# A transformer layer over 16 sequences: the third norm and the first step reordered, and the logarithm of the row sums taken on GpSimd

## The reference

```
x  -> xn = layernorm(x)
q  = xn @ Wq_down.T @ Wq_up.T            c = xn @ Wkv_down.T
k, v per head = c @ k_up[h], c @ v_up[h]
score = q k^T / sqrt(32) - slope[h] * |i - j|, causal
out   = softmax(score) @ v,  then @ Wo.T
x  = x + layernorm(out)
gate, up = layernorm(x) @ w_gu.T  (1408 each; w_gu, w_down decoded from 4-bit codes and scales)
y  = (silu(gate) * up) @ w_down.T;  y = y / rms(y)
x  = x + layernorm(y)
```

## Time and profile before

| | |
|---|---|
| median of 3 runs | 2552.22 us (2552.08 to 2552.81) |
| the profiled execution | 2549.71 us, of which its span is 2547.8 us |
| TensorE (PE) busy | 2445.3 us, 96% of the span |
| VectorE (DVE), ScalarE (ACT), GpSimd (POOL) | 60%, 58%, 23% |
| chain that ended last | PE 80%, DVE 7%, ACT 5%, SP's queue 3% |
| ScalarE table loads | 64 besides the first, 1283 ns each, 4 per step with attention |
| `Ln` of 128x32 | 229 ns, 32 of them |
| `keep_causal` | median 634 ns |
| `h_low` | 1156 ns |

### The profile page before, as it was taken

The page is one execution under the profiler, slowest core; times in us unless marked ns, Lnnn a source line. Parts: engine busy times, 40 slices in busy tenths (PEclk is TensorE's granted clock), DMA queues, the critical chain, the costliest instruction groups (busy, mean ns, idle before and its releaser), DMA issues.

```text
span 2547.8 us, 38721 instructions
## 1 busy us (share of the span) xinstructions
PE 2445.3 (96%) x13372; PEld 1112.6 (44%) x13372; DVE 1523.3 (60%) x4300; ACT 1465.3 (58%) x3927; POOL 591.6 (23%) x648
## 2 busy tenths in 40 slices
PE   6689999999999999999999999999999999999988
PEld 3334444444444444444444444444444444444433
DVE  6856475565646657575665647556564665657442
ACT  3756556474664747566474655747566474756610
POOL 3312313123131221313122131312213122131312
PEclk9699999999999999999999999999999999999999
DMA  5020121201112020121202012120111202012000
GB/s 138 23 49 19 51 50 34 67 18 42 43 43 59 25 72 11 46 50 35 67 18 62 22 51 50 35 67 18 42 43 43 59 24 74 8 48 50 19 17 17
DMA packets 99521, 108.89 MB, mean 43 GB/s; under 512 B 22895, under 2 KB 73199, under 8 KB 99311
## 3 DMA queue, kind: packets, MB, share of 16 engines
q1 hardware_dynamic: 99326, 106.44, 15.9%
HBM read 38.49 MB, written 16.78 MB: 22 GB/s over the span
## 4 chain that ended last, share of the span: by engine, by line
PE 80%; DVE 7%; ACT 5%; SPq 3%; issue 2%; DMA 1%; POOL 1%; DVEq 0%; POOLq 0%
PE dense L338 58%; PE psO L538 6%; PE score L522 4%; SPq L1195 3%; PE psO L338 3%; PE low L505 3%; PE score L505 3%; DVE st_ln L777 2%; ACT arena L719 1%; PE low L522 1%; DVE arena L873 1%; DMA kst<-arena 1%; DVE low L1024 1%; ACT L650 1%; ACT L719 1%
## 5 line engine op out<-in xcount | busy, mean ns | idle before, releaser
L338 PE MATMUL dense<-arena,wgu 128*128 128x512 f16 x4224 | 999.9, 379 | 11.4 <-DVE late L886 10.2
L338 PEld LDWEIGHTS dense<-arena,wgu 128*128 128x128 f16 x4224 | 405.3, 97 | 445.2 <-DVE late L886 17.5
L338 PE MATMUL dense<-wdn,arena 128*128 128x512 f16 x2112 | 533.0, 380 | 2.6 <-POOL arena L1109 2.6
L1109 POOL TENSOR_TENSOR arena<-late,arena 128x512 f16<-128x512 f32 x176 | 203.4, 1156 | 1050.8 <-DVE arena L907 1050.8
L1024 DVE CUSTOM_DVE_ANT_0 low<-low,mmax 128x128 f32<-128x128 f32 (+3 forms) x672 | 278.7, 435 | 260.8 <-PE low L505 257.9
L719 ACT ACTIVATE arena<-score 128x512 f32<-128x512 f32 (+3 forms) x720 | 302.4, 440 | 188.6 <-PE score L522 142.2
L644 ACT ACTIVATE low<-low,ncol 128x128 f32<-128x128 f32 (+3 forms) x672 | 300.1, 447 | 136.7 <-DVE ncol L1024 128.4
L644 ACT ACTIVATE score<-score,ncol 128x384 f32<-128x384 f32 x352 | 214.0, 608 | 169.8 <-DVE ncol L1024 169.4
L338 PEld LDWEIGHTS dense<-wdn,arena 128*128 128x128 f16 x2112 | 199.2, 98 | 186.7 <-issue 11.5
L1024 DVE CUSTOM_DVE_ANT_0 score<-score,mmax 128x384 f32<-128x384 f32 x352 | 214.2, 649 | 100.3 <-PE score L505 100.0
L522 PE MATMUL score<-qst,kst 128*128 128x512 f16 (+3 forms) x784 | 218.6, 306 | 13.8 <-ACT arena L719 12.6
(11 more groups left out here) (138 smaller groups left out, 2874.2 us busy)
## 6 DMA issues: line engine op xcount, KB each, us to landing
qst<-arena SPq DMA_DIRECT2D x384, 64.0 KB, 2.1
kst<-arena SPq DMA_DIRECT2D x192, 128.0 KB, 2.5
xin<-x SPq DMA_DIRECT2D x16, 1024.0 KB, 5.2
late<-x SPq DMA_DIRECT2D x64, 256.0 KB, 2.8
out<-late SPq DMA_DIRECT2D x64, 256.0 KB, 2.0
qst<-mrow SPq DMA_DIRECT2D x96, 8.0 KB, 1.9
wgu<-wo_t SPq DMA_DIRECT2D x1, 1024.0 KB, 7.8
wgu<-wq_down SPq DMA_DIRECT2D x1, 768.0 KB, 4.5
```

Of the source, the lines that this page charges most:

```text
L338: ins = nc.tensor.matmul(dst, w, a, start=first and k == 0, stop=last and k == len(tt) - 1)
L1109: nc.gpsimd.tensor_tensor(ht[:, 1, m, :], tb[:, m % 2, :], ht[:, 0, m, :], ALU.subtract).then_inc(sem["hl"], 1)
```

## The change

1. The logarithm. ScalarE's `Ln` goes. In slots 16 and 40 GpSimd makes a guess from the bits of the row sum (one instruction), ScalarE takes exp(-guess), and GpSimd multiplies the sum with it, evaluates a series for the small rest, and does the three-way split that VectorE did: 15 instructions (8 with two inputs, 7 with one), with 13 waits for the completion of the one before.
2. Third norm. VectorE takes the statistics earlier among the low parts, the low parts of K before those of Q's last two groups, and normalises between these two. `F_FIRST` is 35 in place of 30; the slots get five products less in all.
3. Step 0. The decoding of the gate and up weights moves behind the first low parts, in three pieces; that of the down weights into slot 4; the low part of Wo from VectorE to GpSimd; six of K's twelve stacking DMAs to ScalarE's queue; the order of the first loads changes.

```diff
-LN_SPLIT, LN_ROWS, LN_COPY = (18, 42), (19, 43), (20, 44)
+LN_SUMS, LN_ROWS, LN_COPY = (16, 40), (19, 43), (20, 44)
...
-F_FIRST = 30
+F_FIRST = 35
...
-                def log_sums(part):
-
-                    act.wait_ge(sem["rowsum"], val("rowsum", t, HALF * (part + 1)))
-                    nc.scalar.activation(lcol[:, HALF * part:HALF * part + HALF], scol[:, HALF * part:HALF * part + HALF],
-                                         ACT.Ln).then_inc(sem["ln"], 1)
+                def inverse_guess(part):
+
+                    act.wait_ge(sem["guess"], val("guess", t, part + 1))
+                    nc.scalar.activation(mh32[:, part, :], lcol[:, HALF * part:HALF * part + HALF], ACT.Exp,
+                                         scale=-1.0).then_inc(sem["ln"], 1)
...
+                    if isinstance(t, int) and t == 0:
+
+                        taken(act, t, j["K"] + NG - 1)
+                        stack(nc.scalar, kst, 2, (0, 0, 1), 0, NG, range(2, HG), "kstk")
...
+                if att:
+                    q_low(0)
+                if isinstance(t, int) and t == 0:
+                    decode(2)
+                if ffn:
+                    for i in range(2):
+                        ln3_stats(i)
+                if att:
+                    q_low(1)
+                    k_low(0)
+                if ffn:
+                    ln3_stats(2)
+                if att:
+                    k_low(1)
+                if ffn:
+                    ln3_stats(3)
                     aggregate(t, "ln3", range(NT))
                     ask_rstd("ln3")
                 if att:
-                    if isinstance(t, int) and t == 0:
-                        decode_wo()
                     for g in range(2, NG):
-                        low("Q1", g - 2, qk[:, 1, g, :], HD ** -0.5 * S_QK / (S_X * S_WQ), qk[:, 0, g, :])
+                        k_low(g)
+                if att:
+                    q_low(2)
                 if ffn:
                     dve.wait_ge(sem["rs"], val("rs", t, 2))
                     for i in range(NT):
                         normalise("ln3", xn2[:, i, :], x1[:, i, :], i).then_inc(sem["ln3"], 1)
+                if att:
+                    q_low(3)
...
-                    for part in range(2):
-                        if slot == LN_SPLIT[part]:
-                            lse_split(part)
+                    if isinstance(t, int) and t == 0 and slot == 4:
+                        decode_down()
...
+                def guess_logs(part):
+
+
+                    at = slice(HALF * part, HALF * part + HALF)
+                    pool.wait_ge(sem["rowsum"], val("rowsum", t, HALF * (part + 1)))
+                    nc.gpsimd.tensor_scalar(lcol[:, at], scol[:, at].bitcast(i32), LN2 * 2.0 ** -23, 0.03 - 127 * LN2,
+                                            ALU.mult, ALU.add).then_inc(sem["guess"], 1)
+
+                def finish_logs(part):
+
+                    at = slice(HALF * part, HALF * part + HALF)
+                    h1, h2, h3 = (mh[:, part, HALF * n:HALF * n + HALF] for n in range(3))
+                    log, u, w = lcol[:, at], scol[:, at], mh32[:, part, :]
+                    pool.wait_ge(sem["ln"], val("ln", t, part + 1))
+                    term(nc.gpsimd.tensor_tensor(u, u, w, ALU.mult))
+                    term(nc.gpsimd.tensor_tensor(log, ncol[:, at], log, ALU.subtract))
+                    settled()
+                    term(nc.gpsimd.tensor_scalar(w, u, -1.0, None, ALU.add))
+                    settled()
+                    term(nc.gpsimd.tensor_scalar(u, u, -0.25, 0.25 + 1.0 / 3.0, ALU.mult, ALU.add))
+                    settled()
+                    term(nc.gpsimd.tensor_tensor(u, u, w, ALU.mult))
+                    settled()
+                    for c in (-0.5, 1.0):
+                        term(nc.gpsimd.tensor_scalar(u, u, c, None, ALU.add))
+                        settled()
+                        term(nc.gpsimd.tensor_tensor(u, u, w, ALU.mult))
+                        settled()
+                    term(nc.gpsimd.tensor_tensor(log, log, u, ALU.subtract))
+                    settled()
+                    term(nc.gpsimd.tensor_scalar(log, log, S_SCORE / ROW_MAX, None, ALU.mult))
+                    settled()
+                    term(nc.gpsimd.tensor_scalar(h1, log, 1.0, None, ALU.mult))
+                    settled()
+                    term(nc.gpsimd.tensor_tensor(log, log, h1, ALU.subtract))
+                    settled()
+                    term(nc.gpsimd.tensor_scalar(h2, log, 1.0, None, ALU.mult))
+                    settled()
+                    nc.gpsimd.tensor_tensor(h3, log, h2, ALU.subtract).then_inc(sem["mh"], 1)
...
+                    pool.wait_ge(s_raw_hi, 4)
+                    flat = raw[:, 9 * D:13 * D]
+                    nc.gpsimd.tensor_scalar(flat, flat, S_W, None, ALU.mult).then_inc(s_wo_s, 1)
+                    pool.wait_ge(s_wo_s, 1)
+                    nc.gpsimd.tensor_tensor(wo[:, 1, :, :].rearrange("p a b -> p (a b)"), flat,
+                                            wo[:, 0, :, :].rearrange("p a b -> p (a b)"), ALU.subtract).then_inc(s_wo_lo, 1)
                     for u in range(RING):
                         unit(u)
                 for slot, (low_tiles, exp_tiles) in enumerate(SLOTS):
...
+                    for part in range(2):
+                        if slot == LN_SUMS[part]:
+                            guess_logs(part)
+                            finish_logs(part)
                     for e in exp_tiles:
                         if e % HG == 1 and e > 1:
                             keep_causal(e // HG - 1)
```

More of the change, by code:

```diff
@@ L48 @@
     "po": (0, 0, 4, 4), "out0": (16, 0, 32, 32), "out1": (16, 0, 32, 32), "tanh": (0, 0, 11, 11), "hh": (0, 0, 11, 11),
[1 row of a table removed]
+    "hl": (0, 0, 11, 11), "chain": (8, 12, 49, 41), "guess": (0, 2, 2, 2), "series": (0, 28, 28, 28),
 }
@@ L297, in terms, with stack @@
             return out_
+        def stack(queue, dst, hi, slots, lo_g, hi_g, heads, done):
+            for slot, s in enumerate(slots):
+                for a in heads:
+                    queue.dma_start(
+                        dst[HD * slot:HD * slot + HD, :, :].rearrange("p (g a) l -> p g a l", a=HG)[:, lo_g:hi_g, a, :],
+                        qk[HD * a:HD * a + HD, hi + s, lo_g:hi_g, :]).then_inc(sem[done], 16)
         def unit_src(u):
@@ L737, in step @@
                         if slot == LN_AT[part]:
-                            log_sums(part)
+                            inverse_guess(part)
                     if ffn:
@@ L974, in step, with q_low, k_low, ln3_stats @@
                     link(t, nc.vector.tensor_tensor(ve["ln2"][:, :], mv["ln2"][:, :, 0], rs["ln2"][:, :], ALU.mult))
-                if att:
[L976 to L984, removed]
-                if ffn:
+                def q_low(g):
+                    kind, i = ("Q", g) if g < 2 else ("Q1", g - 2)
+                    low(kind, i, qk[:, 1, g, :], HD ** -0.5 * S_QK / (S_X * S_WQ), qk[:, 0, g, :])
+                def k_low(g):
+                    low("K", g, qk[:, 3, g, :], S_QK / (S_C * S_W), qk[:, 2, g, :])
+                def ln3_stats(i):
+                    dve.wait_ge(sem["add2"], val("add2", t, i + 1))
+                    link(t, nc.vector.bn_stats(st6["ln3"][:, i, :], x1[:, i, :]))
+                if att:
+                    q_low(0)
+                if isinstance(t, int) and t == 0:
+                    decode(2)
+                if ffn:
+                    for i in range(2):
[9 more added lines that the diff above has]
+                    ln3_stats(3)
                     aggregate(t, "ln3", range(NT))
@@ L1116, in y_add, with term, settled @@
                                             ALU.add).then_inc(sem["po"], 1)
+                n_series = [0]
+                def term(ins):
+                    n_series[0] += 1
+                    ins.then_inc(sem["series"], 1)
+                def settled():
+                    pool.wait_ge(sem["series"], val("series", t, n_series[0]))
+                def guess_logs(part):
[3 more added lines that the diff above has]
+                                            ALU.mult, ALU.add).then_inc(sem["guess"], 1)
@@ L1192, in step @@
                         taken(sp, t, last)
-                        for slot, s in enumerate(slots):
-                            for a in range(HG):
-                                sp.dma_start(
-                                    dst[HD * slot:HD * slot + HD, :, :].rearrange("p (g a) l -> p g a l", a=HG)[:, lo_g:hi_g, a, :],
-                                    qk[HD * a:HD * a + HD, hi + s, lo_g:hi_g, :]).then_inc(sem[done], 16)
+                        own = 2 if done == "kstk" and isinstance(t, int) and t == 0 else HG
+                        stack(nc.sync, dst, hi, slots, lo_g, hi_g, range(own), done)
                     for part in range(2):
```

98 lines of the change are left out of this document (52 added, 46 removed), and 1 row of the table COUNTS.

## The result

The changed kernel takes 2612.8 us (median of 4 runs, 2610.9 to 2613.6) against 2552.2 for the one before: a ratio of 1.0238, with a 95% interval from 1.0220 to 1.0255. The forecast was 2590, in a range of 2535 to 2635. The profiled execution spans 2608.7 us (2547.8 before) at a mean granted clock of 0.971 (0.985).

A forecast was written before the change was run, and what follows sets the result against it. PE, busy 149.0 of 151 us a step, was taken to bound the kernel. Steady steps +20, lower clock +20 and step 0 -2 gave +38 on 2552.2: 2590 us, range 2535 to 2635.

The forecast's parts named there:

- rival C: GpSimd's series: waits cost 0.2 each, series 6.3, PE stands 5.5, net +5.5 a step, 2632 us; chance 0.13.
- The stalls of before: PE's idle places at the third norm and behind both logarithms: all go, gaining 2.61 us per step.
- The norm: Third norm: waits of 0.26 after K's products and 0.81 before the transposes go, 1.07 us per step.
- The series: GpSimd's 15-instruction logarithm chain with 13 waits: 4.7 us, from 2.8 lowest to 11.6 highest.
- The stall: PE at values(3), end of slot 41, waits for the select queued behind GpSimd's series: 3.95 us per step.
- The clock: PE's clock falls to half for 4 us at the values(3) stall: 1.3 us a step, +20 in all.
- Net per step: Steps 1 to 15: stall 3.95 less 2.61 gained is +1.34, with the lower clock's 1.3 added, +2.64 us.
- Step 0: Earlier first products -9.5, down decoding +3.9, logarithms +1 and +2.5: sum -2 us, from -9 to +6.
- The first logarithm: Step 0, first half of the logarithm: nothing fills its wait, +1 us.
- A: GpSimd's chain is cheap: series 2.8, PE stands 2.05, clock holds, net -0.56 a step, 2542 us; chance 0.20.
- B: Stall before values(3) as forecast but PE's clock stays full: +20 - 2, 2570 us; chance 0.22.
- D: GpSimd's queue order doesn't bind, values(3) isn't held: -2.61 a step, -41 in all, 2511 us; chance 0.06.

The follow-up runs named there:

- the kernel with the series in two pieces: Changed kernel with Wo's low part and logarithm on VectorE, the first half's series divided between slots 17 and 18: 2508.3 us, ratio to before 0.9837.
- the filler: Changed kernel plus 14 zero-weight 512-column matmuls ahead of values(3) in steps 1 to 15: 2581.5 us, ratio to before 1.0118.
- the short series: Changed kernel with six of the series' fifteen instructions left out, so a coarser logarithm: 2555.6 us, ratio to before 1.0019.

## Why the prediction was right, and where it missed

The mechanism was right: `keep_causal(3)` behind the series in GpSimd's queue, TensorE waiting for it, the clock falling behind the wait. The kernel with the two exchanged shows it. The 22.8 us between 2590 and 2612.8 are sizes, but they are many: 2612.8 lies outside the 2578 to 2606 that I gave this forecast for its own, and a little nearer to rival C's 2632. What tells it from C is the mechanism alone: the waits in the series are 0.08 to 0.09 us and the stall 4.35, not 0.2 and 5.5.

- **The stalls of before.** Forecast 2.61 a step. The kernel with the series in two pieces has practically none and takes 148.45, so before had 151.38 - 148.45 = 2.93. The rest is mostly waits for K's stacking, 0.5 in some steps, which I had not listed.
- **The norm.** Forecast -1.07. As such right, but it also took the first logarithm's 0.84 with it; I had booked that to the table loads. In the sum it makes no difference, for whoever keeps only one half of the change it does.
- **The series.** Forecast 4.7 us; measured from 1203.86 to 1208.88, 5.0. The model was good for two inputs (0.25 for 0.26) and for the waits (0.08); of the seven one-input instructions six take 0.29 to 0.30 for 0.22.
- **The stall.** Forecast 3.95, measured 4.35: 0.3 is the series, and 0.1 is that TensorE was due at `values(3)` at +4.10 (1204.95 + 0.22), not +4.20. The hand-overs ahead of the series took what was forecast (it starts at +2.79).
- **The clock.** Forecast 1.3 a step, from one stretch of step 0; measured 1.78 with the filler. With it the step adds up: 148.45 + 4.35 + 1.78 = 154.58, and 154.66 was measured.
- **Net per step.** Forecast +2.64, measured +3.28: 0.64 x 15 = 10 of the 22.8.
- **Step 0, the term that failed.** Forecast -2 (from -9 to +6), measured +8.1, outside its bounds. The same products laid beside each other, before and after, give the terms. Up to the first maximum: forecast -9.5, measured -2.4. "GpSimd's two passes over 2048 columns lie in the 24.12 us in which it idled" was true of GpSimd and said nothing of VectorE, which they held for 7 us; without them the first maximum comes 6.0 earlier. The decoding in slot 4: priced at its own 3.9, but behind it the kernel is 3.7 late (78.77 for 75.10), so it cost 5 to 6; TensorE stood 4.9 there. The first logarithm: forecast +1, but behind it the kernel is only 2.0 late (110.92 for 108.92), so in sum it gained 1.7, though TensorE waits 2.9 for the series. The second: forecast +2.5, measured +6.1 (2.0 to 8.1); TensorE stands 6.5 us where it stood 3.1.
- **The end.** Behind the last mark it is +6.9, 3.3 of it as in each step. The other 3.6 were in no term; 2.1 of them are the lower clock behind the norm of step 16, which kernels with the new step 0 show in all profiled executions but one, and the two kernels without it do not. Why is open.

Of the rivals, A (a cheap chain, stall 2.05) is what the short series came near to (stall 2.29), at 2555.6 and not at 2542: the clock fell in five steps of 14, each some 2 us longer, and step 0 is 5.0 us longer than before where -2 was forecast. B (the clock stays full, 2570) is what the filler made true of the clock, 2581.5. C's waits of 0.2 are excluded by starts 0.34 apart. D fell: the order on the queue binds.

## What to carry to other kernels

A step that is moved to an idle engine takes its place in that engine's queue: what matters is what stands behind it and who waits for that, not how idle the engine is. Put the short instruction that the busiest engine waits for ahead of the long chain, and cut a chain into pieces that fit the gaps. Time two parts of a change apart before keeping both: here one half was worth -27 us, and the other, as it was placed, hid it and 60 more.

## What the runs showed of the hardware

- Small dependent instructions on 128x32 start 0.34 us apart on the mean on GpSimd (1203.86 to 1208.63, 14 distances) and 0.22 on VectorE (0.18 to 0.19 each), their waits included.
- An instruction of VectorE beside a pass of GpSimd can be held for most of that pass: 4.95 us for 1.62, 4.63 for 0.88.
- On GpSimd the one-input pass over 128x2048 took 6.12 us and the two-input one 4.07, both beside VectorE's work; alone neither was timed.
- The clock behind a stall, in the steady steps of one execution each: full in all behind a stall of 1.32 us (with filler products ahead of it), lower in 5 of 14 behind 2.29 and in 5 of 14 behind 1.83 and 0.53 close together, lower in all behind 4.35. Between these it isn't the length alone that decides.
- A stall of 4.35 us cost 6.1: the 1.78 behind it can be had back with products that compute nothing.
